# Float32 one-hots that carry the edge weights, and a first pass with its products in PSUM

## What is computed

```python
# layer 0
msgs = x[src] * edge_weight[:, None]
out = segment_sum(msgs, dst)
# layer 1: a gated message by a small MLP of edge_attr, summed by src
# layer 2: softmax over the edges of a node
ex = exp(logits - seg_max[dst])
a = ex / segment_sum(ex, dst)[dst]
rst = elu(segment_sum(soft_label[src] * a[:, None], dst))
# layer 3: twice
x = segment_sum(x[src] * edge_weight[:, None], dst)
avg = avg + x * scale
```

## Time and profile before

| | us |
|---|---|
| median of 3 runs | 14637.14 (14630.46 to 14647.33) |
| the profiled execution's own time | 14613.11 |
| its span | 14611.4 |
| first pass | about 125 to 3330 |
| second pass | about 3430 to 6600 |
| light passes | about 6680 to 9295, 9340 to 11950, 11970 to 14600 |

### The profile page before, as it was taken

One profiled execution on the slowest core, in us unless ns is written; L12 is line 12 of the kernel. 1 busy time (PEld: TensorE's weight loads), 2 busy tenths in 40 slices (PEclk: granted clock), 3 DMA queues, 4 the chain that ended last, 5 costly groups with the idle time before them and its releaser, 6 DMA issues. The chain is left out here.

```text
span 14611.4 us, 229268 instructions
## 1 busy us (share of the span) xinstructions
PE 6196.8 (42%) x41742; PEld 4830.5 (33%) x41743; DVE 4470.0 (31%) x18451; ACT 3889.5 (27%) x13481; POOL 9177.6 (63%) x8348
## 2 busy tenths in 40 slices
PE   4444444444555555542333333333333333333333
PEld 2222222223444444432333333233333333333333
DVE  5444444445444444443111111211111121111111
ACT  3444444442333333321111111111111111111111
POOL 5555555556888888874666666566666656666665
DMA  4333333334555555551111111111111111111111
GB/s 117 104 104 102 103 101 102 101 101 57 62 62 61 62 61 61 62 87 35 16 16 16 16 16 16 20 16 16 16 16 16 16 22 16 16 16 16 16 16 21
DMA packets 812412, 690.95 MB, mean 47 GB/s; under 512 B 418932, under 2 KB 671220, under 8 KB 810119
## 3 DMA queue, kind: packets, MB, share of 16 engines
q0 software_dynamic: 452736, 234.14, 14.8%
q1 hardware_dynamic: 357051, 450.30, 11.6%
q10 hardware_dynamic: 2588, 6.12, 0.1%
HBM read 572.77 MB, written 117.06 MB: 47 GB/s over the span
## 5 line engine op out<-in xcount | busy, mean ns | idle before, releaser
L708 POOL DMA_INDIRECT table<-table,idx x4992 | 4822.8, 966 | 3230.0 <-ACT idx L715 1704.7
L786 PE MATMUL psum_acc<-table 128*128 128x48 f32 (+1 forms) x12288 | 2951.1, 417 | 5142.0 <-DVE acc L748 2400.8
L786 PEld LDWEIGHTS psum_acc<-table 128*128 128x128 f32 x12288 | 2734.4, 328 | 5358.7 <-issue 5315.2
L1045 POOL DMA_INDIRECT sums<-rows,idx x1664 | 2621.0, 1575 | 592.8 <-issue 431.5
L476 POOL DMA_INDIRECT rows<-table,idx x1668 | 1673.1, 1003 | 1550.8 <-ACT idx L528 1015.9
L759 DVE TENSOR_TENSOR table<-iota,dstf 128x512 f32 x1536 | 1064.5, 693 | 3025.5 <-issue 2113.7
L715 ACT CAST idx<-srow 128x4 int32 (+1 forms) x1266 | 243.4, 193 | 6334.1 <-DVEq L767 4216.7
L748 DVE TENSOR_TENSOR acc<-acc,psum_acc x1539 | 312.3, 203 | 3467.4 <-remote 2411.0
L961 PE MATMUL psum_exp<-table,onet 128*128 x6144 | 431.4, 219 | 1368.9 <-DVE onet L880 1135.9
L676 PE MATMUL psum_acc<-parts,onehot 128*128 128x48 bf16 x6144 | 338.4, 215 | 1574.5 <-DVE onehot L619 1386.4
L728 ACT ACTIVATE table<-table,w 128x48 f32<-128x48 f32 x3328 | 840.9, 324 | 26.8 <-DMA table<-table,idx 16.8
(11 more groups left out here) (171 smaller groups left out, 7187.4 us busy)
## 6 DMA issues: line engine op xcount, KB each, us to landing
drow<-rows_dram SPq DMA_DIRECT2D x832, 128.0 KB
lrow<-in_logit_rows SPq DMA_DIRECT2D x416, 256.0 KB
table<-table,idx POOLq DMA_INDIRECT x4992
srcrow<-rows_dram SPq DMA_DIRECT2D x416, 128.0 KB
hid_dram<-hid SPq DMA_DIRECT2D x416, 96.0 KB
hid<-hid_dram SPq DMA_DIRECT2D x416, 96.0 KB
rows<-table,idx POOLq DMA_INDIRECT x1668
sums<-rows,idx POOLq DMA_INDIRECT x1664
```

Source lines behind the costliest of these rows:

```text
L708: pool.indirect_dma_start(out=ring[:, u, 0:cols], out_offset=None, in_=src_table, in_offset=bass.IndirectOffsetOnAxis(ap=idx[:, u:u + 1], ...
L786: last = nc.tensor.matmul(psum_acc[:, ds(win & 1, 1), 0:cols].rearrange("p r c -> p (r c)"), hot[:, j % 2, u, :], ring[:, j * G + u, 0:col ...
L1045: pool.indirect_dma_start(out=sums[c], out_offset=bass.IndirectOffsetOnAxis(ap=idx[:, slot:slot + 1], axis=0), in_=rows[:, slot, 0:CS], in ...
```

## The change

In the light passes ScalarE's multiplications and their semaphore go; ScalarE only stages indices. VectorE makes each tile's one-hot by itself: `tensor_scalar` compares the block's node numbers with the tile's destination (a scalar a partition) and multiplies by the tile's weight (another), so `hot` holds the weight in place of 1. TensorE waits for the rows' landing itself. In the first pass the bfloat16 one-hot is also made by four `tensor_scalar`, without a weight, and `prod`, `rest` and `pen` move into PSUM banks that are free in that pass (`psum_comb` and the second bank of `psum_acc`); `prod` and `rest` in SBUF stay for the second pass, which is not changed.

```diff
--- before.py
+++ after.py
@@ -128,7 +128,6 @@
         far = sb("far", [P, NBW])
         dots = sb("dots", [P, G, GE])
         adaptg = sb("adaptg", [P, G])
-        pen = scratch[:, 0:GW]
         junk = scratch[:, GW:2 * GW]
 
         def ps(name, shape):
@@ -464,7 +463,10 @@
             s_hid = sem(name + "_hid")
             s_hidout = [sem(f"{name}_hidout{r}") for r in range(2)]
             width = src_table.shape[1]
-            
+            prod0 = psum_comb[0][:, 0:2 * G * cols].rearrange("p (r u c) -> p r u c", r=2, u=G)
+            rest0 = psum_comb[1][:, 0:G * cols].rearrange("p (u c) -> p u c", u=G)
+            pen0 = psum_acc[:, 1, :]
+
             with nc.Block() as block:
                 @block.gpsimd
                 def _(pool):
@@ -530,19 +532,19 @@
                     def part0(g, par):
                         act.wait_ge(s_prod32, g + 1)
                         act.sem_inc(s_seen, 1)
-                        nc.scalar.copy(parts[:, par, :, 0, 0:cols], prod[:, par, :, 0:cols]).then_inc(s_part0, 1)
+                        nc.scalar.copy(parts[:, par, :, 0, 0:cols], prod0[:, par, :, :]).then_inc(s_part0, 1)
 
                     def part1(g, par):
                         act.wait_ge(s_rest, g + 1)
                         act.sem_inc(s_seen, 1)
-                        nc.scalar.copy(parts[:, par, :, 1, 0:cols], rest[:, :, 0:cols]).then_inc(s_part1, 1)
+                        nc.scalar.copy(parts[:, par, :, 1, 0:cols], rest0[:, :, :]).then_inc(s_part1, 1)
 
                     def weigh(i, j):
 
                         act.wait_ge(s_rows[j % RING], i * (GB // RING * 16 * G) + (j // RING + 1) * 16 * G)
                         act.sem_inc(s_seen, 1)
                         for u in range(G):
-                            last = nc.scalar.activation(prod[:, j % 2, u, 0:cols], rows[:, j % RING * G + u, 0:cols], ACT.Copy,
+                            last = nc.scalar.activation(prod0[:, j % 2, u, :], rows[:, j % RING * G + u, 0:cols], ACT.Copy,
                                                         scale=weights[:, ds(i * U + (j * G + u), 1)])
                         last.then_inc(s_prod32, 1)
 
@@ -566,7 +568,7 @@
                                 act.wait_ge(s_maxed, win)
                                 act.sem_inc(s_seen, 1)
 
-                                nc.scalar.activation(pen[:, :], drow[:, j % 2, :], ACT.Abs, scale=BIG, bias=far[:, ds(k, 1)]).then_inc(s_pen, 1)
+                                nc.scalar.activation(pen0, drow[:, j % 2, :], ACT.Abs, scale=BIG, bias=far[:, ds(k, 1)]).then_inc(s_pen, 1)
                                 act.reg_add(wn_act, wn_act, 1)
 
                             act.wait_ge(s_free, i * GB + (j + RING))
@@ -600,11 +602,11 @@
 
                     def leave(g, par):
                         dve.wait_ge(s_part0, g + 1)
-                        nv.tensor_tensor(rest[:, :, 0:cols], prod[:, par, :, 0:cols], parts[:, par, :, 0, 0:cols], ALU.subtract).then_inc(s_rest, 1)
+                        nv.tensor_tensor(rest0[:, :, :], prod0[:, par, :, :], parts[:, par, :, 0, 0:cols], ALU.subtract).then_inc(s_rest, 1)
 
                     def part2(g, par):
                         dve.wait_ge(s_part1, g + 1)
-                        nv.tensor_tensor(parts[:, par, :, 2, 0:cols], rest[:, :, 0:cols], parts[:, par, :, 1, 0:cols], ALU.subtract).then_inc(s_part2, 1)
+                        nv.tensor_tensor(parts[:, par, :, 2, 0:cols], rest0[:, :, :], parts[:, par, :, 1, 0:cols], ALU.subtract).then_inc(s_part2, 1)
 
                     leave(0, 0)
                     with dve.Fori(0, TURNS) as i:
@@ -616,9 +618,10 @@
                             dve.sem_inc(s_seen, 1)
                             with dve.Fori(*spans[j]) as k:
                                 win = dve.snap(wn_dve)
-                                nv.tensor_tensor(onehot[:, :, :], iota[:, ds(k * P, P)].unsqueeze(1).to_broadcast([P, G, P]),
-                                                 dstf[:, ds(i * U + j * G, G)].unsqueeze(2).to_broadcast([P, G, P]),
-                                                 ALU.is_equal).then_inc(s_hot, 1)
+                                for u in range(G):
+                                    last = nv.tensor_scalar(onehot[:, u, :], iota[:, ds(k * P, P)], dstf[:, ds(i * U + (j * G + u), 1)], None,
+                                                            ALU.is_equal)
+                                last.then_inc(s_hot, 1)
 
                                 dve.wait_ge(s_exp, win)
                                 dve.sem_inc(s_seen, 1)
@@ -627,7 +630,7 @@
                                 dve.wait_ge(s_pen, win)
                                 dve.wait_ge(s_maxed, win)
                                 dve.sem_inc(s_seen, 1)
-                                nv.tensor_tensor_reduce(out=junk, in0=lrow[:, j % 2, :], in1=pen[:, :], scale=1.0, scalar=-BIG,
+                                nv.tensor_tensor_reduce(out=junk, in0=lrow[:, j % 2, :], in1=pen0, scale=1.0, scalar=-BIG,
                                                         op0=ALU.subtract, op1=ALU.max, accum_out=wmax[:, :]).then_inc(s_wmax, 1)
 
                                 dve.wait_ge(s_added, win)
@@ -693,7 +696,6 @@
             s_idx = sem(name + "_idx")
             s_done = sem(name + "_done")
             s_clear = sem(name + "_clear")
-            s_weighed = sem(name + "_weighed")
             s_flushed = sem(name + "_flushed")
             arrived = order * TURNS * 16 * G
 
@@ -722,12 +724,6 @@
                             act.sem_inc(s_seen, 1)
                             stage((j + LEAD) % DEPTH, i * U + (j + LEAD) * G)
 
-                            act.wait_ge(s_landed_rows[j], i * (16 * G) + (arrived + 16 * G))
-                            act.sem_inc(s_seen, 1)
-                            for u in range(G):
-                                last = nc.scalar.activation(ring[:, j * G + u, 0:cols], ring[:, j * G + u, 0:cols], ACT.Copy,
-                                                            scale=weights[:, ds(i * U + (j * G + u), 1)])
-                            last.then_inc(s_weighed, 1)
 
                 @block.vector
                 def _(dve):
@@ -756,10 +752,11 @@
                                 win = dve.snap(wn_dve)
                                 dve.wait_ge(s_picked, dve.snap(room_dve))
                                 dve.sem_inc(s_seen, 1)
-                                nv.tensor_tensor(hot[:, j % 2, :, :],
-                                                 iota[:, ds(k * P, P)].unsqueeze(1).to_broadcast([P, G, P]),
-                                                 dstf[:, ds(i * U + j * G, G)].unsqueeze(2).to_broadcast([P, G, P]),
-                                                 ALU.is_equal).then_inc(s_spread, 1)
+                                for u in range(G):
+                                    t = i * U + (j * G + u)
+                                    last = nv.tensor_scalar(hot[:, j % 2, u, :], iota[:, ds(k * P, P)], dstf[:, ds(t, 1)], weights[:, ds(t, 1)],
+                                                            ALU.is_equal, ALU.mult)
+                                last.then_inc(s_spread, 1)
                                 keep(win, s_kept)
                                 dve.reg_mov(before_dve, k)
                                 dve.reg_add(wn_dve, wn_dve, 1)
@@ -775,7 +772,7 @@
                     with pe.Fori(0, TURNS) as i:
                         spans = load_ranges(pe, i)
                         for j in range(GB):
-                            pe.wait_ge(s_weighed, i * GB + (j + 1))
+                            pe.wait_ge(s_landed_rows[j], i * (16 * G) + (arrived + 16 * G))
                             pe.sem_inc(s_seen, 1)
                             with pe.Fori(*spans[j]) as k:
                                 win = pe.snap(wn_pe)
```

## The result

The changed kernel takes **14,890.8 us** in the median (14,869.5 to 14,894.8) against 14,636.3 us of the kernel before beside it: ratio 1.0172, 95% interval 1.0155 to 1.0188, **254 us slower**. The forecast was 568 us slower (15,205), inside a range of 14,430 to 15,800: the sign was right, the size was not. The profiled execution took 14,891.0 us, 278 more than that of before.

A forecast was written before the change was run, and what follows sets the result against it. GpSimd's gathers, pausing for idx behind VectorE's late instructions, were taken as the bound. Terms +40 + 581 + 98 - 150 = +569 on 14613 gave 15182, with 24 us 15,205 us; range 14,430 to 15,800.

The forecast's parts named there:

- the first rival: VectorE's code length costs nothing and only GpSimd's gathers gain: -208 us, 14,430 us; chance 0.20.
- the late rows: VectorE's register adds and moves, usually 40 and 36 ns, up to 1,396 and 722; read as instructions arriving late while gathers flow.
- part 4: GpSimd's gathers, all passes: stretched less as VectorE reads fewer SBUF operands; -150 us taken, bounds 0 and -208.
- part 3's light term: Light passes: VectorE's code grows from 120 to 168 instructions a turn, giving 114 more pauses of 5.1 us, +581 us.
- part 2: Light passes: VectorE's one-hot becomes four float32 operations, at most 1.0 us a window; +40 us taken, bounds -28 and +86.
- The rival by which the pauses stay as many and only get longer: Light passes: pause-ending bursts get longer, one in four by a slow window; +299 less 150, 14,785 us; chance 0.15.
- part 1: Light passes: ScalarE's weighing goes; idx staging does not wait behind it, so 0 us.
- The lower bound, -370: Light passes: the gain from dropping ScalarE's weighing if every pause began with it, up to 1.3 us each.
- The rival by which the engines share what supplies them: Shared supply, so ScalarE's lost code counts: light passes -160, first pass +98, gathers -150, 14,425 us; chance 0.08.
- part 5: First pass: PSUM in place of SBUF changes operations between pause and idx by 20 ns either way; 0 us taken.
- part 3's first-pass term: First pass: six more VectorE instructions a window body; half of a possible +196 us taken, +98 us.
- Its bound of 1.0 us a window: Light passes: four short one-hot operations take at most 4 x 0.249 = 1.0 us a window.

The follow-up runs named there:

- e15: Kernel before with PSUM operands in the first pass; light passes: VectorE weighs, weighing left out, six semaphore instructions a window body; late chip, 14,641.6 us against 14,625.5.
- e16: Kernel before with six semaphore instructions a window body (first pass, first light pass), tile-by-tile one-hot (second), VectorE weighing (third); late chip, 14,676.3 us against 14,625.5.
- e18: Kernel before with first-pass products and rests in PSUM, penalties in SBUF, and VectorE weighing in the light passes; prompt chip, 12,083.5 us.
- e14: Kernel before with first-pass products, rests and penalties in PSUM, one-hot and light passes as before; prompt chip, ratio 0.9952, -57 us.
- e13: Kernel before with VectorE weighing a group in one multiply in the light passes, in place of ScalarE's four; prompt chip, ratio 0.9976, -31 us.
- e9: Kernel before with the light one-hot made tile by tile, ScalarE still weighing; late chip, 14,810.1 us, ratio 1.0124, +185 us.
- e10: Kernel before with ScalarE's light-pass weighing left out (weights not computed), one-hot as before; late chip, 14,365.4 us, ratio 0.9820, -260 us.

## Why the prediction was right and wrong

**Right: what bounds the kernel.** GpSimd's wait for idx behind a late VectorE set the end, and more VectorE code made it later. The six semaphore instructions show this by themselves on a late chip, +45 us in e15 and +53 in e16 for a light pass. That it is a condition of the chip, absent on four of six, the trace of one chip could not tell; I took it for the kernel's nature. By the rule of the Trainium skill that I held as the first rival (Runtime: NRT & Kernel Launch, "Instruction fetch mechanics": the fetch is mostly hidden; the section excepts taken branches that leave its two-page window, which the prediction did not weigh), the change would have gained what the gathers gain; on the prompt chips it did, -168 us with gathers 169 us shorter, and on the late ones it did not, +254 us with gathers 189 us shorter. Whether the late rows are late code is my reading of them still; no run shows the fetch.

**Right: part 4.** The gathers gave 189 of the possible 208 us; I took 150. The Trainium skill's rule that I weighed there (SBUF — State Buffer, "SBUF: two separate sides") agrees: from e18 to e14 the first pass differs only in the penalties, whose reading by VectorE (and writing by ScalarE) moves from SBUF to PSUM, and 1010 ns became 976. e13 sets a limit to it: an added operation with two SBUF inputs went with gathers 6 ns shorter.

**Wrong: part 3's light term, "285 x 0.40 = 114 more, x 5.1 = +581".** This is the step that failed most. The six instructions a body were as counted, five register operations a window on L757 in place of two. The price of a pause was right too, 5.09 us before and after. What failed is that the number of pauses would grow with the length of the code, one per 65 instructions: the changed kernel has 305 in place of 285, 20 more and not 114, and e9, with the longer code and ScalarE still weighing, 333. The same number of instructions without operations cost +45 and +53 us a pass, by my estimate some 150 us over three passes (3 x 50), a quarter of the term. All of GpSimd's new idle time in e9 is 270 us, under half of the term, with part 2's operations in it; less the gathers' 83 that is the +185 measured. The rival by which the pauses stay as many and only get longer, to 6 us, fell too: their length did not change.

**Wrong: part 1, "the row at 12143.77 has idx ahead of it, so 0".** The reading of the row was right, and it holds for all 285 pauses. What was wrong is the conclusion that the weighing then costs nothing: without it e10 took 260 us less, its pauses 0.8 us shorter and 22 fewer, though no multiplication lay inside one. The lower bound, -370, was nearer to e10's -260 than the 0, by luck: its picture, each pause beginning with weighing, is nowhere in the trace. With the one-hot tile by tile less of it is left (e9 to after: 2,657 to 2,618 in the middle pass, and 105 us over the three), so the light passes' +74 are the one-hot's +179 less these 105. The rival by which the engines share what supplies them, which got 0.08, isn't excluded by this: it had ScalarE's shorter code as a gain of 160 us in the light passes, and e10 changes no code of VectorE. Its total of 14,425 us was wrong all the same, and a run with a longer code of ScalarE alone, which could tell, is missing.

**Wrong: part 5, "0", and part 3's first-pass term, +98.** Together +98 for a pass that lost 201 after a relief of 99. GpSimd's idle time in the pass rose by 299 us (1,550.8 to 1,849.8); e15's PSUM part alone made 239 of it (1,789.7), so the tile-by-tile one-hot some 60. My sum had the first on neither side: the cost of PSUM was looked for in the duration of single operations, where there is next to none (ScalarE's casts took 321 to 324 ns against 354 to 357 from SBUF, VectorE's first subtraction 366 against 358). Why it costs stays open.

**Part 2, +40**, was of the right kind and isn't measured alone: e9 holds it together with the code (270 us less the 150 above would leave it some 120, an estimate). Its bound of 1.0 us a window held for the form without a weight (e16: 497 us busy for 512 windows, 0.97) and was low for the one with it (1,831 for 1,536, 1.19).

## What to carry to other kernels

Before a wait is put down to the kernel, look whether the same program shows it on another chip: here 2.5 of 14.6 ms and the sign of this change hung on that. Where an engine's pauses alternate with runs, do not scale their number with one quantity that happens to fit two passes; make a small run that changes that quantity alone, as the six semaphore instructions do. Look at the length of the waits before counting them, since a view may name a releaser for a usual step. That work lies beside a pause in every row does not make it free: leaving out ScalarE's weighing was worth 260 us. And where VectorE's operands may stretch GpSimd's gathers, try the widest operation with two SBUF inputs first; here it held 55 of 65 us.

No one version is best on both kinds. On prompt chips the change is (-168 us). On late ones VectorE's weighing with everything else as before is the best seen, -88 and -91 us a pass in e15 and e16, some 14,366 us by my estimate (14,636 - 3 x 90); as a whole kernel it ran on prompt chips alone (-31 us).

## What the runs showed of the hardware that I had not expected

- Two conditions of chip: a register move and an addition of VectorE that take up to 0.717 and 0.725 us on some, at most 43 and 45 ns on others, under the same program; the kernel before takes 14.63 or 12.12 ms. What makes a chip late isn't known.
- On a prompt chip VectorE's semaphore instructions, which touch no data, changed the mean gather by +19 ns (light passes) and -22 ns (first pass).
- A 128x128 `tensor_scalar` from uint16 to float32 with two scalars a partition took 354 ns in the mean, with one scalar 299; four overlap to 1.19 and 0.97 us, against 0.69 us for one 128x512 `tensor_tensor`.
- Moving one reduction's second input to PSUM relieved the gathers by 55 us on a prompt chip, and the PSUM part as a whole lost 139 us on a late one.
